# Input rows of the later attention units turned by transfers and VectorE blocks instead of TensorE

## What is computed

```python
def layer(x, gamma, beta, wq, bq, wk, bk, wv, bv, wp, bp):
    xn = group_norm(x, gamma, beta)          # 32 groups of 8 channels
    q, k, v = xn @ wq + bq, xn @ wk + bk, xn @ wv + bv
    attn = softmax(q @ k.T / sqrt(256))      # 1024 x 1024 for each image
    return (attn @ v) @ wp + bp + x
out = layer(layer(x, *weights0), *weights1)
```

## Time and profile before

| what | value |
|---|---|
| median of three runs | 264.88 us |
| the profiled execution, whole | 265.16 us |
| its span, first to last instruction | 263.3 us |
| TensorE (PE) busy | 257.6 us, 98% |
| VectorE (DVE) busy | 178.2 us, 68% |
| ScalarE (ACT) busy | 151.3 us, 57% |
| GpSimd (POOL) busy | 110.5 us, 42% |

### The profile page before, as it was taken

One profiled execution on the slowest core, in us unless ns is written; L12 is line 12 of the kernel. 1 busy time (PEld: TensorE's weight loads), 2 busy tenths in 40 slices (PEclk: granted clock), 3 DMA queues, 4 the chain that ended last, 5 costly groups with the idle time before them and its releaser, 6 DMA issues.

```text
span 263.3 us, 4614 instructions
## 1 busy us (share of the span) xinstructions
PE 257.6 (98%) x1662; PEld 233.8 (89%) x1662; DVE 178.2 (68%) x437; ACT 151.3 (57%) x295; POOL 110.5 (42%) x111
## 2 busy tenths in 40 slices
PE   7799999999999999999999999999999999999995
PEld 6688889889998899889998899889998899889995
DVE  0688877886983677389876677479966667257603
ACT  3575544699984539535567529544577439542900
POOL 2010901185769019310575609510474809500940
PEclk9999999999999999999999999999999999999999
DMA  6960000000000000000000000000010000100102
GB/s 211 339 212 0 0 4 0 0 0 2 0 1 4 0 2 0 0 2 1 0 4 0 0 2 0 0 2 20 24 40 0 4 20 20 40 2 20 42 20 80
DMA packets 6989, 7.37 MB, mean 28 GB/s; under 512 B 556, under 2 KB 6712, under 8 KB 6968
## 3 DMA queue, kind: packets, MB, share of 16 engines
q1 hardware_dynamic: 6944, 7.08, 8.0%
q10 hardware_dynamic: 24, 0.01, 0.0%
HBM read 4.99 MB, written 2.10 MB: 27 GB/s over the span
## 4 chain that ended last, share of the span: by engine, by line
PE 91%; DVE 5%; DMA 2%; SPq 1%; ACT 0%; issue 0%; DVEq 0%
PE ring L942 11%; PE ring L944 11%; PE ring L943 11%; PE ring L981 11%; PE ring L983 11%; PE ring L982 11%; PE ring L928 3%; PE ring L929 3%; PE ring L930 3%; PE ring L915 3%; PE ring L917 2%; PE ring L916 2%; PE Z L831 2%; DVE S L637 2%; DMA xnat<-in_x 2%; PE X L974 1%
## 5 line engine op out<-in xcount | busy, mean ns | idle before, releaser
L291 POOL TENSOR_TENSOR P_lo<-S,P_hi 128x512 fp32r<-128x512 f32 x64 | 82.9, 1314 | 93.5 <-ACT S L406 93.3
L981 PE MATMUL ring<-V,P_hi 128*128 128x258 f32 x256 | 73.7, 288 | 0.0
L983 PE MATMUL ring<-V,P_lo 128*128 128x258 f32 x256 | 72.2, 282 | 0.0
L982 PE MATMUL ring<-V,P_hi 128*128 128x256 f32 x256 | 72.2, 282 | 0.0
L398 ACT COPY S<-ring 128x512 f32<-128x512 f32 x64 | 37.3, 590 | 44.2 <-PE ring L944 40.9
L405 ACT ACTIVATE P_hi<-S 128x512 fp32r<-128x512 f32 x64 | 40.2, 628 | 37.2 <-DVE S L637 37.2
L942 PE MATMUL ring<-t_hi,xn_lo 128*128 128x512 f32 x128 | 51.5, 402 | 0.0
L944 PE MATMUL ring<-t_hi,xn_hi 128*128 128x512 f32 x128 | 50.1, 391 | 0.0
L943 PE MATMUL ring<-t_lo,xn_hi 128*128 128x512 f32 x128 | 49.9, 390 | 0.0
L982 PEld LDWEIGHTS ring<-V,P_hi 128*128 128x128 f32 x256 | 48.4, 189 | 0.5
L981 PEld LDWEIGHTS ring<-V,P_hi 128*128 128x128 f32 x256 | 48.4, 189 | 0.5
(11 more groups left out here) (103 smaller groups left out, 342.0 us busy)
## 6 DMA issues: line engine op xcount, KB each, us to landing
xnat<-in_x SPq DMA_DIRECT2D x8, 256.0 KB, 6.2
out<-xnat SPq DMA_DIRECT2D x16, 128.0 KB, 1.7
wide<-in_vectors SPq DMA_DIRECT2D x2, 384.0 KB, 6.6
w_wq<-in_L_conv_wq SPq DMA_DIRECT2D x2, 256.0 KB, 4.4
w_wk<-in_L_conv_wk SPq DMA_DIRECT2D x2, 256.0 KB, 4.6
w_wv<-in_L_conv_wv SPq DMA_DIRECT2D x2, 256.0 KB, 6.0
w_wp<-in_L_conv_wp SPq DMA_DIRECT2D x1, 256.0 KB, 5.8
w_wp<-in_L_conv_wo SPq DMA_DIRECT2D x1, 256.0 KB, 6.3
```

Source lines behind the costliest of these rows:

```text
L291: nc.gpsimd.tensor_tensor(P_lo[:, exp_of(c, kb), :], S[:, tile_of(c, kb), :], P_hi[:, exp_of(c, kb), :].bitcast(F32), ALU.subtract).then_i ...
L981: nc.tensor.matmul(bank[:, 0:C + 2], P_hi[:, tile, mine], v[:, kb, 0:C + 2], start=(kb == 0), stop=False)
L982: nc.tensor.matmul(bank[:, 0:C], P_hi[:, tile, mine], v[:, kb, C + 2:VX], start=False, stop=False)
L983: last = nc.tensor.matmul(bank[:, 0:C + 2], P_lo[:, tile, mine], v[:, kb, 0:C + 2], start=False, stop=(kb == NB - 1))
```

## The change

For units 1, 2 and 3 the rows are no longer turned by TensorE. SP moves them with transfers from SBUF to SBUF: for each row tile i of unit v, 16 transfers, each from 32 partitions of `xnat` (group g) to 32 partitions of a new buffer `moved` (group a), 64 pieces of 32 floats. That is 8 x 16 = 128 transfers for a unit and 384 in all. When both tiles of a pair have landed (semaphore `mv_x[v, i]` at 256), VectorE transposes `moved` in 32x32 blocks into `xraw`, one 128x512 instruction for a pair, 12 in all, as the first step of `statistics_of`. The transfers of units 2 and 3 wait for the `output` of their row tile and for the VectorE transpose of the unit before that read the same place of `moved`. ScalarE's 12 copies and TensorE's 12 groups of transposes of these units go away.

Steps are also reordered. Unit 1: statistics of pairs 0, 1, 2 after running maxima 3, 5, 7 of chunk 0, those of pair 3 ahead of `v_low(0, 4)`, group matmuls within the scores of chunk 1. Units 2 and 3: pairs 0 and 1 after running maxima 4 and 7 of the first chunk, pair 2 after running maximum 1 of the second, pair 3 after its running maximum 4; `mean_of_groups` after score tile 6 and `variance_of_groups` after tile 7; the map and all of `normalise` after `query_shift(second)`; `t_product` of the next unit one output tile later. The core of the diff:

```diff
+            def move_rows(v, i):
+                if v < IMAGES:
+                    sp.wait_ge(ld_x[v][i // 2], 16)
+                else:
+                    sp.wait_ge(dv_O, (v - IMAGES) * NB + i + 1)
+                if v > 1:
+                    sp.wait_ge(dv_turn, (v - 2) * NR + i // 2 + 1)
+                for g in range(QUARTERS):
+                    rows = xnat[g * SQ:(g + 1) * SQ, v % IMAGES, i, :].rearrange("p (k a c) -> p a k c", k=KC, c=SQ)
+                    for a in range(QUARTERS):
+                        sp.dma_start(moved[a * SQ:(a + 1) * SQ, :, i, g, :], rows[:, a]).then_inc(mv_x[v, i], 16)
+
+            for v in range(1, UNITS):
+                for i in range(NB):
+                    move_rows(v, i)
...
             def statistics_of(v, r):
-                dve.wait_ge(ac_xT, v * NR + r + 1)
+                if v == 0:
+                    dve.wait_ge(ac_xT, r + 1)
+                else:
+                    for i in (2 * r, 2 * r + 1):
+                        dve.wait_ge(mv_x[v, i], MOVED)
+                    nc.vector.transpose(xraw[:, :, 2 * r * P:2 * (r + 1) * P],
+                                        moved[:, :, 2 * r:2 * r + 2].rearrange("p k i g c -> p k (i g c)")
+                                        ).then_inc(dv_turn, 1)
+                    dve.wait_ge(dv_turn, (v - 1) * NR + r + 1)
...
                 running_max(0, kb)
-                if kb <= NR:
-                    statistics_of(1, kb - 1)
-                if kb == NR:
-                    channel_statistics(1)
-            group_deviation(1)
+                if kb in (3, 5, 7):
+                    statistics_of(1, kb // 2 - 1)
             for m in range(QB):
                 v_low(0, m)
                 if m == 2:
                     query_maxima(0)
             query_shift(0)
-            variance(1)
+            statistics_of(1, 3)
+            channel_statistics(1)
             for m in range(QB, NB):
                 v_low(0, m)
...
-                    if kb == 0 and more:
-                        next_rows(u + 1, 3)
-                    if more and kb == 2:
+                    if more and kb == 6:
                         mean_of_groups(u + 1)
-                    if more and kb == 4:
+                    if more and kb == 7:
                         variance_of_groups(u + 1)
 
-                attention(first, second, next_first_half, lambda: None)
+                attention(first, second, lambda: None, next_first_half)
```

More of the change, by code:

```diff
@@ L49, in two_attention_layers @@
     TILES = 12
+    MOVED = 16 * QUARTERS ** 2
     P_TILES = 16
@@ L161, in two_attention_layers @@
         ld_w = {(l, k): sem(f"ld_{k}{l}") for l in range(LAYERS) for k in ("wq", "wk", "wv", "wp")}
+        mv_x = {(v, i): sem(f"mv_x{v}_{i}") for v in range(1, UNITS) for i in range(NB)}
         ld_vec = sem("ld_vec")
@@ L304, in _ @@
                     residual(u, i)
-                if u == 0:
-                    power(1)
                 for kb in range(NB):
                     p_low(2 * u, kb)
+                    if u == 0 and kb == 2:
+                        power(1)
                 if 0 < u < UNITS - 1:
@@ L466, in _ @@
                 for kb in range(6):
-                    if more and kb in (2, 3):
-                        t_high(u + 1, 0, kb - 2)
+                    if more and kb in (3, 4):
+                        t_high(u + 1, 0, kb - 3)
                     exponentials(second, kb)
@@ L711, in _ @@
                     running_max(first, kb)
-                    if more and kb in (3, 6):
+                    if more and kb in (4, 7):
                         statistics_of(u + 1, kb // 3 - 1)
@@ L727, in _ @@
                 output(before, 2)
+                output(before, 3)
+                running_max(second, 1)
                 if more:
                     statistics_of(u + 1, 2)
-                output(before, 3)
+                for kb in range(2, 5):
+                    running_max(second, kb)
                 if more:
@@ L734, in _ @@
                     channel_statistics(u + 1)
-                running_max(second, 1)
-                running_max(second, 2)
+                running_max(second, 5)
+                running_max(second, 6)
                 if more:
                     group_deviation(u + 1)
-                running_max(second, 3)
+                running_max(second, 7)
                 if more:
                     variance(u + 1)
-                running_max(second, 4)
+                query_maxima(second)
+                query_shift(second)
                 if more:
                     affine_map(u + 1)
[L745 to L756, removed]
                 output(first, 0)
                 if more:
+                    normalise(u + 1)
                     xn_low(u + 1, 0)
@@ L770, in _ @@
                     shifted(second, 2)
+                    output(first, 2)
+                    shifted(second, 3)
                     t_low(u + 1, 0, 0)
-                    shifted(second, 3)
+                    shifted(second, 4)
                     t_low(u + 1, 0, 1)
-                    output(first, 2)
-                    shifted(second, 4)
+                    output(first, 3)
                     shifted(second, 5)
-                    output(first, 3)
                 else:
@@ L1033, in _ @@
                 scores(1, kb)
+                if kb == 2:
+                    mean_of_groups(1)
+                if kb == 5:
+                    variance_of_groups(1)
             for kb in range(NB):
```

67 lines of the change are left out of this document (24 added, 43 removed).

## The result

The changed kernel takes 415.75 us (median of 4 runs, 414.21 to 417.74) where the kernel before takes 265.04: a ratio of 1.569, interval 1.562 to 1.577. The direction was forecast, the size was not: 295.5 us was forecast, and the range ended at 335.

A forecast was written before the change was run, and what follows sets the result against it. TensorE, 98% busy, was taken to bound the kernel, with SP's issue of 384 transfers deciding after the change. 265.2 + 17.0 + 9.4 + 3.9 for units 1, 2 and 3 gave 295.5 us, range 265 to 335.

The forecast's parts named there:

- whatever leaves TensorE's stream shortens the run: TensorE, 98% busy: removing twelve groups of transposes at 0.45 us saves 5.3 us, provided nothing makes TensorE wait.
- VectorE's transposes: Twelve 128x512 transposes added on VectorE, taken at 0.6 us each, 7.2 us in all; without waits only late ones count.
- The no-wait time of the changed kernel: Whole run without any wait for transfers: 259.9 + 1.2 = about 261 us.
- The rule of the Trainium skill named ahead of the result: Transposes: sends 128x128 to TensorE, giving 390 ns there and 311 ns on VectorE, in blocks only; speaks against the change.
- SP's price: SP's queue, 384 transfers: 0.35 us each, bounds 0.24 and 0.52; 5.6 us a row tile, 45 us a unit.
- the nearest rows: SP's issue price taken from a store, 128 pieces, 0.33 us, and a weight load, 256 pieces, 0.47 us.
- The sum by stages: Delays from late transfers: unit 1 +17.0 us, unit 2 +9.4, unit 3 +3.9, on top of 265.2.
- tiles 0 to 3 have time: Unit 3: transfers of the first four row tiles cause no delay; only tiles 4 to 7 add 3.9 us.
- Issue as dear as a load's: Rival on SP's queue: 0.42 to 0.52 us a transfer, 318 to 350 us; chance 0.13.
- The DMA engines bound it: Rival: SBUF-to-SBUF packets of 128 bytes take over 70 ns; at 85 ns the run takes 320 us; chance 0.08.
- Issue is cheap: Rival on SP's queue: 0.20 us or less a transfer, every pair in time, about 261 us; chance 0.14.
- The clock, which I left out of the sum: TensorE idle some 10 us in unit 1 might fall to half clock, losing half a microsecond per microsecond of work.

The follow-up runs named there:

- e7: Kernel before, its order; only pairs 0 to 2 of units 2 and 3 turned by VectorE, rows through HBM in 5 transfers a pair: 262.5 us, ratio 0.991.
- e9: Kernel of e7 with unit 1 also turned by VectorE, rows read from the input in HBM, mean_of_groups(1) behind values(0, 0): 261.9 us, ratio 0.987.
- e6: As e2, but with all steps in the order of the kernel before; the transposes stay on VectorE: 264.9 us, ratio 1.000.
- e2: Changed kernel without the 384 transfers; eight loads from HBM fill moved once, so the rows are not the right ones: 268.1 us, ratio 1.012.
- e1: Separate kernel that computes nothing, issuing series of 12 transfers of one shape each: 0.60 us an issue SBUF to SBUF, 0.43 from HBM for 128 x 256.
- e8: Second kernel that computes nothing, with further transfer shapes on SP: 0.42 us an issue for 32 x 64 floats from HBM, 0.59 for 32 x 2 x 32.
- e4: Changed kernel with moved laid out by row tile, one transfer for both tiles of a pair, 192 instead of 384: 306.5 us, ratio 1.157.
- e5: Changed kernel with idle multiplications on TensorE ahead of its long waits, about as many as fit, to keep its clock up: 420.7 us.

## Why the prediction was wrong

**What bounds the kernel.** The chain on TensorE was read rightly, but the step "whatever leaves TensorE's stream shortens the run" was wrong in part. In units 2 and 3 a group removed is worth 0.45 us (e7: 2.7 us forecast, 2.5 measured). In unit 1 it is worth next to nothing (e9), because VectorE binds right behind TensorE in the scores of chunk 0: its waits there were 2.9 us before, four transposes take 2.8 of them, and nothing is left for starting 1.8 us earlier. A stream that is 98% busy hides a second one right behind it.

**VectorE's transposes.** 0.71 us each, not 0.6: 1.3 us on twelve, small. That they fit into VectorE's gaps failed in unit 1, and e6 shows the price: 264.9 us where the kernel before without its twelve groups would be 259.7, part of it by the clock that fell behind the wait for VectorE. The no-wait time of the changed kernel, 261 in my sum, is 268.1 (e2). The rule of the Trainium skill named ahead of the result ("VectorE: DVE Perf Modes", section "Rules for kernel authors"), to turn 128x128 on TensorE, was right for this kernel as it was built; e7 shows that with cheap transfers and free places on VectorE the other way can win 1%.

**SP's price: the step that failed.** I took 0.35 us a transfer with bounds of 0.24 and 0.52, from rows with HBM on one side; it is 0.65. The step was "the nearest rows": they were near in size and far in kind. No row of the kernel before has SBUF on both sides, and the line through 128 and 256 pieces that took the price down to 0.26 had no ground, since e1 finds no dependence on pieces at all. The pieces of 128 bytes are a second such difference: with HBM on one side they cost 0.59 to 0.63 us too (e1, e8), and no row of the kernel before has them. The upper bound was set at the dearest row of another kind, and the range inherited it. The Trainium skill, "DMA: Bandwidth & Descriptors", section "Anatomy of one DMA — SWDGE (gpsimd) path", puts the sequencer's dispatch at about 50 ns and descriptor generation at "small, variable"; that is written for GpSimd's queue, and on SP's queue the measurement here is twelve times the 50 ns. The Trainium skill, on the same page in "Rules for kernel authors", says to coalesce many small transfers, which e4 and e7 bear out.

**The sum by stages.** Its mechanism was right and can be checked with the measured price. By its own slopes (1.28, 1.28 and 0.64 us for 0.01 us of issue), 0.655 us (21 us for the 32 transfers of a pair) instead of 0.35 turns 17.0, 26.4 and 30.3 us behind in chunks 1, 3 and 5 into 56.0, 104.4 and 127.8; measured are 58.9, 106.6 and 147.3. Unit 1 is 2.9 us short: the map ahead of `query_maxima(1)` takes 3.7 us (116.3 to 120.0) where the sum had 1.2, with three small operations at 0.8 to 1.2 us instead of 0.16. Unit 2 comes within 0.7 us, in part by luck: from the transpose of pair 3 to `query_maxima(3)` it takes 7.9 us where the sum has 6.3, and smaller terms make up for it. Unit 3 is 17.3 us short: "tiles 0 to 3 have time" was true at 5.6 us a row tile and false at 10.4; VectorE waits 13.3 us for pair 1 there, 14.6 us of delay between chunks 3 and 4. The other 2.7 us lie behind pair 3, 9.1 us instead of 6.3, and the half clock there is worth 3 us by the estimate above. A term that is zero at the taken price need not be zero along the whole range; I extended the sum with the slope of the terms that were not. Another 1.9 us come behind chunk 5, where e2 has them too (the new order). 265.2 + 127.8 + 2.9 - 0.6 + 17.3 + 1.9 = 414.5, against 414.2 of the profiled execution.

**The rivals.** *Issue as dear as a load's* was the right family, with too low an upper end. *The DMA engines bound it* fell: 10.4% of their time, and e4 takes off 109 of the 150.7 us lost without moving a byte less. *Issue is cheap* fell by the first row. The clock, which I left out of the sum, did fall to 0.5 in the waits. The Trainium skill has it so for an idle TensorE ("TensorE: Matmul & The Clock Gate", section "Part 1: The HAM clock gate"). It is on the path behind each unit's last landing, for up to 8 us by estimate, and e5 didn't test it there.

**What showed it.** SP's queue is solid from 15 to 99 us, TensorE is idle at 41 to 62, 66 to 84 and 91 to 103 us, and again ahead of `mean_of_groups` in units 2 and 3 (22.6 and 22.8 us). The first two come earlier than I had them, because pairs 1 and 2 of unit 1 hold `running_max` and `query_shift` before pair 3 holds anything.

## What to carry to other kernels

Count the instructions on the queue that issues transfers as you count those of a compute engine: number times price, against the time between the first moment they may start and the moment the last is wanted. Take the price from a row with the same memory at both ends and pieces of the same size, or measure it alone first; it costs one run. When a term of a sum is zero at the value you took, ask at which value it begins, and let the range know. And when an experiment changes a mean, such as the clock's, look at the stretch that is on the path: the mean can rise while that stretch stays as it was.

## What the runs showed of the hardware that I had not expected

- Issuing a transfer from SBUF to SBUF takes 0.59 to 0.60 us (median) on SP's queue in nearly every shape tried (0.62 for 128 x 2 x 32 floats) and 0.62 us on ScalarE's, from 1 partition x 64 floats to 128 x 256; from or to HBM 0.42 to 0.47 us, but 0.59 to 0.63 us in pieces of 128 bytes.
- Behind a wait of 2.7 us TensorE's granted clock was 0.50 for some 3.3 us in e6, and 258-column matmuls started 0.215 us apart instead of 0.12.
- A 128x512 float32 transpose in 32x32 blocks takes 0.71 us on VectorE.
- VectorE's two-column operations with two SBUF operands take 1.2 us instead of 0.16 while GpSimd's `p_low` runs without a gap.
- 64 KB in 128-byte pieces, written to HBM shortly before, come back 2.6 us after the issue.
